# Turning the experts' inner values: one 32-bit array, or two 16-bit parts, through the transpose of a graph network and mixture-of-experts kernel

## What is computed

```
hid = relu(einsum('nd,edf->enf', h2, W1) + b1[:, None, :])     # 768 -> 3072
y = einsum('enf,efd->end', hid, W2) + b2[:, None, :]           # 3072 -> 768
moe = einsum('ne,end->nd', combine, y)
```

## Time and profile before

| | |
|---|---|
| median of three executions | 1099.87 us |
| the profiled execution | 1102.97 us |
| its span, first to last instruction | 1101.2 us |
| mean granted TensorE clock | 0.978 of full speed |
| TensorE busy with matmuls | 1037.7 us (94%) |
| VectorE busy | 729.8 us (66%) |
| ScalarE busy | 570.8 us (52%) |
| experts' blocks | from 618.26 us to the last second product, about 1093 us |

### The profile page before, as it was taken

The page is one execution under the profiler, slowest core; times in us unless marked ns, Lnnn a source line. Parts: engine busy times, 40 slices in busy tenths (PEclk is TensorE's granted clock), DMA queues, the critical chain, the costliest instruction groups (busy, mean ns, idle before and its releaser), DMA issues.

```text
span 1101.2 us, 19073 instructions
## 1 busy us (share of the span) xinstructions
PE 1037.7 (94%) x6167; PEld 651.7 (59%) x6168; DVE 729.8 (66%) x1300; ACT 570.8 (52%) x782; POOL 184.9 (17%) x186
## 2 busy tenths in 40 slices
PE   5999999999999999989998699999999999999997
PEld 3555558756766775566777255555555555555554
DVE  6677768595666654189976888911129898989411
ACT  2666769513240344178834576811128778777310
POOL 3000040040205331072001301110103120211000
PEclk9999999999999999989998699999999999999999
DMA  8300030301507500030026699940009999999100
GB/s 312 106 0 0 1 115 1 115 1 59 112 1 156 87 1 1 1 112 2 2 86 201 244 390 325 351 168 0 25 0 352 375 375 360 390 359 390 72 4 3
DMA packets 92263, 155.60 MB, mean 141 GB/s; under 512 B 36507, under 2 KB 36587, under 8 KB 92214
## 3 DMA queue, kind: packets, MB, share of 16 engines
q1 hardware_dynamic: 89814, 149.20, 39.2%
q0 software_dynamic: 2400, 5.77, 1.5%
HBM read 153.21 MB, written 7.77 MB: 146 GB/s over the span
## 4 chain that ended last, share of the span: by engine, by line
PE 75%; DVE 10%; issue 5%; ACT 4%; DMA 2%; POOL 1%; DVEq 1%; SPq 0%; ACTq 0%; POOLq 0%
PE psum L1519 29%; PE psum L1794 18%; PE psum L1769 17%; PE psum L1778 2%; PE psum L1507 2%; PE psum L1557 2%; DVE area L1380 2%; DMA low<-in_L_ffn_W_dram 2%; DVE smalls L1021 1%; PE psum L1765 1%; PE psum L1677 1%; DVE area L1351 1%; DVE area L1108 1%; ACT low L915 1%; PE psum L1621 1%
## 5 line engine op out<-in xcount | busy, mean ns | idle before, releaser
L1380 DVE TENSOR_TENSOR area<-low,area 128x1536 f16<-128x1536 f32 x144 | 245.9, 1753 | 13.3 <-ACT area L970 13.1
L1519 PE MATMUL psum<-area,low 128*125 128x512 f16 (+4 forms) x1068 | 236.9, 381 | 1.3 <-DVE low L1253 1.3
L1769 PE MATMUL psum<-area,low 128*128 128x512 f16 x972 | 220.7, 381 | 0.0
L1794 PE MATMUL psum<-area,low 128*128 128x384 f16 x1296 | 219.3, 327 | 0.0
L970 ACT ACTIVATE area<-low 128x1536 f16<-128x1536 f32 x138 | 200.3, 1484 | 34.0 <-DMA low<-in_L_ffn_W_dram 28.1
L1519 PE MATMUL psum<-area 125*128 125x64 f16 (+10 forms) x1452 | 196.1, 289 | 10.1 <-DVE area L1351 5.5
L1519 PEld LDWEIGHTS psum<-area,low 128*125 128x125 f16 (+2 forms) x1068 | 136.4, 141 | 92.4 <-issue 53.1
L1794 PEld LDWEIGHTS psum<-area,low 128*128 128x128 f16 x1296 | 127.3, 98 | 80.7 <-issue 1.7
L1519 PEld LDWEIGHTS psum<-area 125*128 125x128 f16 (+3 forms) x1452 | 126.7, 122 | 62.8 <-issue 12.3
L1769 PEld LDWEIGHTS psum<-area,low 128*128 128x128 f16 x972 | 95.5, 98 | 113.9 <-issue 3.0
L981 ACT ACTIVATE low<-psum 128x512 f32<-128x512 f32 x54 | 31.9, 591 | 161.5 <-PE psum L1769 158.1
(11 more groups left out here) (246 smaller groups left out, 1183.9 us busy)
## 6 DMA issues: line engine op xcount, KB each, us to landing
low<-in_L_ffn_W_dram SPq DMA_DIRECT2D x144, 768.0 KB, 7.7
area<-in_L_gnn_W_dram SPq DMA_DIRECT2D x2, 3072.0 KB, 11.9
area<-in_L_gnn_Wr_dram SPq DMA_DIRECT2D x2, 3072.0 KB, 15.7
low<-in_x_dram SPq DMA_DIRECT2D x10, 336.0 KB
area<-in_L_ffn_Wv_dram SPq DMA_DIRECT2D x6, 384.0 KB, 6.2
area<-in_L_ffn_Wq_dram SPq DMA_DIRECT2D x6, 384.0 KB, 7.1
area<-in_L_ffn_Wk_dram SPq DMA_DIRECT2D x6, 384.0 KB, 6.1
area<-in_L_ffn_Wp_dram SPq DMA_DIRECT2D x2, 1152.0 KB, 6.7
```

What stands on the lines that cost most here:

```text
L1380: dve.tensor_tensor(low_, raw_view(u), high_, ALU.subtract).then_inc(low_ok, 1)
L1519: ins = pe.matmul(place(name)[0:parts, at:at + w], left(q), right(q)[:, at:at + w], start=(q == 0), stop=(q == k - 1))
L1769: ins = pe.matmul(psum[:, (c % 2) * BANK:(c % 2 + 1) * BANK], ht[x_][:, k, :], w1_s[c][w_][:, k, :], start=False, stop=(k == KD - 1 and x_ ...
L1794: ins = pe.matmul(psum[:, (4 + q) * BANK:(4 + q) * BANK + D // 2], hidT[c % 2][x_][:, j, :], w2_s[c][w_][:, j, q * D // 2:(q + 1) * D // 2 ...
```

## The change

ACT's ReLU now writes a 16-bit value into `hid[c][0]`, the high part, and DVE makes the low part `hid[c][1]` from the same PSUM bank ahead of the transpose: the larger of PSUM and 0, minus the high part, in one instruction. TensorE transposes both 16-bit parts, in eight pieces of 128x128 in place of four, against a 16-bit identity, into one PSUM bank that now holds 1024 16-bit values per partition. ACT copies that bank in one instruction of 1024 values into `hidT_both[c]`. DVE has no work behind the transpose any more. The transpose now waits for DVE's low part (`hid_cp`), and the second product for ACT's copy (`hid_relu`). One copy ahead of the blocks makes `ident16`.

```
-        hid = [carve(CW) for _ in range(2)]
-        hidT = [[v3(carve(CW // 2).bitcast(F16), CK) for _ in range(2)] for _ in range(2)]
+        hid = [[carve(CW // 2).bitcast(F16) for _ in range(2)] for _ in range(2)]
+        hidT_both = [carve(CW).bitcast(F16) for _ in range(2)]
+        hidT = [[v3(both[:, q * CW:(q + 1) * CW], CK) for q in range(2)] for both in hidT_both]
...
-            act.sem_inc(hid_cp, 2)
+            act.sem_inc(hid_relu, 2)
...
-                    act.activation(hid[s_ % 2], psum[:, (s_ % 2) * BANK:(s_ % 2 + 1) * BANK],
-                                   ACT.Relu).then_inc(hid_cp, 1)
+                    act.activation(hid[s_ % 2][0], psum[:, (s_ % 2) * BANK:(s_ % 2 + 1) * BANK],
+                                   ACT.Relu).then_inc(hidhi_ok, 1)
                 if 1 <= s_ <= C:
                     c = s_ - 1
                     act.wait_ge(hid_tr, b * C + (c + 3))
                     act.wait_ge(hid_used, b * C + (C + c - 1))
-                    act.activation(hidT[c % 2][0], v3(psum[:, (2 + c % 2) * BANK:(3 + c % 2) * BANK], CK),
-                                   ACT.Copy).then_inc(hidhi_ok, 1)
+                    act.activation(hidT_both[c % 2], psum[:, (2 + c % 2) * BANK:(3 + c % 2) * BANK].bitcast(F16),
+                                   ACT.Copy).then_inc(hid_relu, 1)
...
+            dve.tensor_copy(ident16, ident).then_inc(b1_ok, 1)
...
-                if 1 <= s_ <= C:
-                    c = s_ - 1
-                    dve.wait_ge(hidhi_ok, b * C + (c + 1))
-                    dve.tensor_tensor(hidT[c % 2][1], v3(psum[:, (2 + c % 2) * BANK:(3 + c % 2) * BANK], CK),
-                                      hidT[c % 2][0], ALU.subtract).then_inc(hid_relu, 1)
-                    if c == C - 1:
-                        tokens_low(b + 1)
+                if s_ < C:
+                    dve.wait_ge(hidhi_ok, b * C + (s_ + 1))
+                    dve.scalar_tensor_tensor(out=hid[s_ % 2][1], in0=psum[:, (s_ % 2) * BANK:(s_ % 2 + 1) * BANK],
+                                             scalar=0.0, in1=hid[s_ % 2][0], op0=ALU.max,
+                                             op1=ALU.subtract).then_inc(hid_cp, 1)
+                if s_ == C:
+                    tokens_low(b + 1)
...
                     pe.wait_ge(hid_cp, b * C + (c + 3))
                     pe.wait_ge(hid_relu, b * C + (c + 1))
-                    for j in range(CK):
-                        ins = pe.transpose(psum[:, (2 + c % 2) * BANK + j * BR:(2 + c % 2) * BANK + (j + 1) * BR],
-                                           hid[c % 2][:, j * 128:(j + 1) * 128], ident)
+                    turned_out = psum[:, (2 + c % 2) * BANK:(3 + c % 2) * BANK].bitcast(F16)
+                    for q in range(2):
+                        for j in range(CK):
+                            ins = pe.transpose(turned_out[:, (q * CK + j) * BR:(q * CK + j + 1) * BR],
+                                               hid[c % 2][q][:, j * 128:(j + 1) * 128], ident16)
                     ins.then_inc(hid_tr, 1)
```

More of the change, by code:

```diff
@@ L317, in gnn_moe_kernel @@
         b1_parts = T_[0:112, 4400:4400 + CW // 2].bitcast(F16)
+        ident16 = T_[:, 4400 + CW // 2 + E * C // 2:4400 + CW // 2 + E * C // 2 + 64].bitcast(F16)
+        assert 4400 + CW // 2 + E * C // 2 + 64 <= TW
         b1_pick = T_[0:112, 4400 + CW // 2:4400 + CW // 2 + E * C // 2].bitcast(F16)
@@ L1447, in _ @@
             dve.tensor_copy(nblocks, nblk_sum[0:1, E - 1:E]).then_inc(routed, 1)
-            dve.sem_inc(hid_relu, 2)
+            dve.sem_inc(hid_cp, 2)
             link(dve.tensor_scalar(base8, start, float(BR), None, ALU.mult))
@@ L1753, in _ @@
             pe.sem_inc(hid_used, C)
-            pe.wait_ge(b1_ok, 3)
+            pe.wait_ge(b1_ok, 4)
             with pe.Fori(0, blocks) as b:
```

## The result

| | before | after |
|---|---|---|
| median | 1100.05 us (12 runs) | 1102.47 us (12 runs) |
| ratio, 95% interval | | 1.0026 (1.0015 to 1.0037) |
| profiled execution, span | 1101.2 us | 1100.5 us |
| mean granted clock | 0.978 | 0.980 |

What follows compares the result with a forecast made beforehand. PE was taken to bound the kernel, busy 49.42 of 50 us where new weights arrive. PE's pieces 0.6, four blocks 1.8 and blocks 4 and 7 1.8 made +4.2 us on 1099.87: 1104.1 us, range 1098.5 to 1110.

Steps and rivals of the forecast that it cites:

- the signs of being right: Pieces 56 ns apart, 1.1 us idle ahead of chunk 1's transpose in blocks 4 to 7, block 0's first transpose waiting 1.5.
- PE's own work: On PE, 54 transposes of eight 16-bit pieces replace four 32-bit ones, +0.01 us each, +0.6 us.
- the 113-column row: On PE, 16-bit matmuls of 113 columns, own weight loads, 0.050 us apart; from it some 0.056 us per 128-column piece.
- The rival of the loads: On PE, weight loads of 98 ns don't overlap in transposes: +18.6 us, 1122 us with the waits; chance 0.09.
- Blocks 4 and 7: DVE works without a gap from the block before, so a shift is passed on: second product +0.88 us, twice, +1.8 us.
- DVE had the data long before: At chunk 0's low part in blocks 4 and 5: late only because three weight units' low parts stand ahead on DVE.
- Blocks 5 and 6: DVE's units in stage 0 absorb small shifts; the second product starts 0.45 us later in each.
- 4 x 0.45: Blocks 0, 1, 5 and 6: the second product starts 0.45 us later in each, +1.8 us.
- Is chunk 0's low part in time at the head of stage 0?: Block 4: yes, by 0.1 us; block 0: no, its transpose waits 1.5 us, which only moves an existing wait forward.
- Block 0: Stage 1 of block 0: the second product starts 0.45 us later, the transpose being done after the wait.
- the rival: Blocks 0 and 1: longer idle makes the clock fall once more, 1.4 us lost, 1105.5 us; chance 0.18.
- Block 1: Stage 1 of block 1: the second product starts 0.45 us later, the transpose being done after the wait.
- The rival of the freed second product: Chunk 0's second product in stage 1 no longer waits, today's waits of 5.5 us go: 1095.0 us; chance 0.06.

Runs made afterwards that it cites:

- the two runs meant to measure its share alone: The joined wait plus a useless 328-column copy ahead of ACT's copies: in every stage 1104.86 us, ratio 1.0049; in stage 5 alone 1104.23 us, ratio 1.0046.
- the spread wait: The kernel before, where chunk 0's transpose also waits for DVE's unit 8: 1098.51 us, ratio 0.9988.
- the joined wait: The kernel before, where chunk 1's transpose also waits for chunk 0's low part, no work or order changed: 1104.35 us, ratio 1.0035.

## Why the prediction was right, and which terms missed

The forecast was +4.2 us, 1104.1 us, inside what a measurement can tell but on the slow side; 1102.47 us came, +2.9 by the ratio. The time was in the range, and the signs of being right came: pieces 56 ns apart, DVE's new low part ahead of chunk 1's transpose as what ends the wait, no wait ahead of the bias, 0.69 and 1.02 us for the two changed instructions. The idle time was 0.9 us where 1.1 was expected, and 1.28 ahead of block 0's first transpose for 1.5. By its steps:

- **PE's own work**, +0.6 us: blocks 2, 3 and 8 lose 0.07 us each, 0.012 per transpose, 0.6 us in all. The 56 ns estimated from the 113-column row was exact. With that the rule of the Trainium skill ("TensorE: Matmul & The Clock Gate", section "Back-to-back issue gap", 81 ns for load and matmul at 128 columns) is not what this kernel shows: 56 ns, also when the pieces are doubled. The rival of the loads is out.
- **Blocks 4 and 7**, "+0.88 us, twice": measured +0.96 and +1.31, of which the pieces are 0.07 each. The wait is where it was foretold, and in block 4 it has the size; block 7's excess is chunk 0's transpose, 0.33 us late (next step). Chunk 1's low part ends 0.50 us later in block 4 (13.73 against 13.23), for an expected 0.43. DVE's row starts 0.4 us later in the new kernel, which is the length that ACT's copy gained; but the two runs meant to measure its share alone met other waits, so that the copy is the cause is argued from those rows and not shown. One reading was wrong: "DVE had the data long before". ACT's copy had ended 0.87 us before DVE's piece in block 4 and 0.74 in block 5, so DVE's units hold it up by no more than that, and with a unit less ahead of it the piece waits for ACT.
- **Blocks 5 and 6**, "4 x 0.45": measured +1.01 and +0.65, too little foretold. The step that failed is "Is chunk 0's low part in time at the head of stage 0?", which was answered with yes from the row of DVE in block 4. In blocks 5, 6 and 7 the transpose that needs it was 0.62, 0.17 and 0.33 us late. The four table reads ahead of it were missed. Before, they were hidden: in block 5 they ended at 892.0, and the next unit had its turn at 892.65. The new piece at the head of the block is the first that must come behind them in a hurry. One read less gave 1.44 us back over blocks 4 to 7.
- **Block 0**, +0.45: measured -1.45. The sum left the clock as it was, and the rival had the sign wrong: the clock was to fall once more, because the idle times would grow. Instead the one fall that was there went away, because the first transpose's wait now takes its part of the idle time a whole product earlier. That is 1.7 us. The wait itself grew less than foretold: the bias of the second product starts 18.49 us into the block, against 18.35, so 0.14 us for 0.45.
- **Block 1**, +0.45: measured -0.70. In the kernel before, ACT's units wait there for the weights' DMA (2.15 and 0.46 us of idle), and DVE's for ACT. How long differed between the profiled kernels: the same block took 52.88 us with the spread wait and 52.96 with the joined one, not 53.35. In the changed kernel it is at 52.65, which is also what blocks 4, 5 and 7 take in the kernel with one table read less. Why the weights came earlier wasn't tried; this part is open.

So the places and the mechanism of the wait were right, and that the sum came so near is in part luck. By the blocks of the two profiles +4.2 us was forecast and +2.0 measured: blocks 0 and 1 came out 3.2 us below their terms, 1.7 of it the clock, and blocks 5 to 7 1.0 us above theirs, mostly by the table reads. The wide range took in what was left. Its upper end is also a little short by its own working: 1107.7 + 3.1 is 1110.8, not 1110. The rival of the freed second product was wrong for the reason given: the order, not the subtraction, held PE up. That was also the better lever, and it works without the change.

## What to carry to other kernels

Before moving a piece from behind an engine's work to ahead of it, look at what stands in front of the piece in its own engine's row: in every block with new weights of the changed kernel the data for chunk 1's low part had been ready for 1.2 to 2.4 us when the piece started. If a wait is there already, ask what work was being done inside it; making that work depend on the awaited piece adds its length, 0.44 us a block in the kernel with the joined wait. And the first instruction of a loop round pays for what the sequencer does at its head, which a piece with slack hides.

## What was not expected of the hardware

- A wait added ahead of a transpose made the kernel 0.12% faster (0.9988, 0.9977 to 0.9999). Idle times of 1.19 and 1.30 us with only a transpose between them were followed by 3.4 us at a granted clock of 0.50 (24 matmuls in 5.44 us); idle times of 2.00 and 1.73 us with a first product of 4.1 us between them were not (4.07 us). How idle time must lie for the clock to fall isn't settled by these profiles.
- A read of one number from memory into a register costs DVE's sequencer 0.71 us here (0.30 the load, the rest the steps around it), and four of them at a block's head were left uncovered where the row behind them was in a hurry: 0.64 us idle in block 5.
- Transposes of 128x128 16-bit values, each with its own load of 98 ns, start 56 ns apart; a 32-bit one takes 109 ns. So two 16-bit parts of a 128x512 piece take PE 0.45 us, one 32-bit array 0.44.
